# One stage for layer norm, routing, ranks, the row table and ten shared groups, with a fixed table region for each expert

## The reference

```python
x = x + scan_layer(layernorm(x))            # unchanged by this change
xt = layernorm(x)                           # 8192 x 256
scores = softmax(xt @ gate_w.T)             # 15 experts
topk_w, topk_idx = top_k(scores, 3); topk_w /= sum(topk_w) + 1e-20
h = xt @ fc1_w[e].T + fc1_b[e]; xh, g = h[:256], h[256:]
y = sum over the 3 chosen e of topk_w * ((gelu(g) * xh * mult[e]) @ fc2_w[e].T + fc2_b[e])
hs = xt @ s_fc1_w.T + s_fc1_b; xs, gs = hs[:512], hs[512:]
ys = (gelu(gs) * xs * s_mult) @ s_fc2_w.T + s_fc2_b      # the shared expert, every token
x = x + y + ys
```

## Time and profile before

| | us |
|---|---|
| median of 3 runs (1834.9 to 1839.58) | 1835.92 |
| the profiled execution | 1849.06 |
| its span, first to last instruction | 1847.4 |
| routing, first load of `x2` to 724 | 107 |
| ranks, 724 to 752 | 28 |
| shared groups 0 to 9, 752 to 1043 | 291 |
| experts, 1043 to about 1690 | 647 |

### The profile page before, as it was taken

One profiled execution on the slowest core, in us unless ns is written; L12 is line 12 of the kernel. 1 busy time (PEld: TensorE's weight loads), 2 busy tenths in 40 slices (PEclk: granted clock), 3 DMA queues, 4 the chain that ended last, 5 costly groups with the idle time before them and its releaser, 6 DMA issues. The chain is left out here.

```text
span 1847.4 us, 25112 instructions
## 1 busy us (share of the span) xinstructions
PE 1490.6 (81%) x5738; PEld 928.8 (50%) x5738; DVE 1089.6 (59%) x2054; ACT 842.3 (46%) x1420; POOL 1118.8 (61%) x1021
## 2 busy tenths in 40 slices
PE   6883766667666595496888699999999999995997
PEld 2332444444443494253544466666666666663564
DVE  5655999999999486521211444444444444442698
ACT  6887988988998110111111133333333333332210
POOL 6887887888886231576767166666666666662000
PEclk9996888888889555697988899999999999997998
DMA  4433233332231461586873222222222222224895
GB/s 135 141 109 138 71 124 114 126 124 100 97 126 57 150 196 45 132 146 103 154 135 61 59 86 86 89 87 88 88 87 89 86 86 89 89 87 166 290 346 210
DMA packets 138089, 221.23 MB, mean 120 GB/s; under 512 B 21021, under 2 KB 103173, under 8 KB 137989
## 3 DMA queue, kind: packets, MB, share of 16 engines
q1 hardware_dynamic: 100053, 138.17, 24.4%
q0 software_dynamic: 27840, 60.96, 10.5%
q10 hardware_dynamic: 10096, 20.86, 6.0%
HBM read 153.13 MB, written 66.79 MB: 119 GB/s over the span
## 5 line engine op out<-in xcount | busy, mean ns | idle before, releaser
L1697 PE MATMUL bank<-arena_dt,xgT 128*128 x832 | 393.6, 596 | 0.1
L741 POOL TENSOR_TENSOR state<-arena_x,b_all 128x1024 f32<-128x1024 f32 x128 | 301.5, 2365 | 69.7 <-issue 66.3
L765 PE MATMUL bank<-ident,state 128*128 128x128 f32 x1024 | 189.0, 321 | 165.6 <-ACT scaled L678 73.2
L1656 POOL DMA_INDIRECT choice_out<-ye,ids x208 | 205.3, 987 | 163.2 <-DVE ye L1796 159.8
L820 DVE TENSOR_TENSOR_SCAN state<-bank,state 128x1024 f32<-128x1024 f32 x128 | 291.6, 2279 | 5.0 <-POOL state L741 4.9
L1782 DVE TENSOR_TENSOR hid<-bank,arena_x 128x512 f32<-128x512 f32 x208 | 143.9, 692 | 250.2 <-PE bank L1697 250.2
L1647 POOL DMA_INDIRECT xg<-x_norm,tokens x208 | 201.2, 967 | 101.8 <-issue 60.9
L765 PEld LDWEIGHTS bank<-ident,state 128*128 128x128 f32 x1024 | 131.5, 162 | 225.8 <-DVE state L820 123.3
L1536 POOL DMA_INDIRECT row_choice<-choice_all,row_i x192 | 188.9, 984 | 72.2 <-issue 55.1
L1762 ACT ACTIVATE gluT<-bank 128x256 f32<-128x256 f32 x208 | 80.0, 385 | 321.9 <-PE bank L1706 321.9
L1714 PE MATMUL bank<-arena_x,gluT 128*128 x832 | 213.9, 380 | 0.0
(11 more groups left out here) (160 smaller groups left out, 2245.3 us busy)
## 6 DMA issues: line engine op xcount, KB each, us to landing
b_all<-bc_rows SPq DMA_DIRECT2D x64, 512.0 KB, 3.5
arena_x<-choice_out SPq DMA_DIRECT2D x64, 384.0 KB, 7.7
xin<-in_x SPq DMA_DIRECT2D x16, 512.0 KB, 3.9
x_skip<-xin SPq DMA_DIRECT2D x16, 512.0 KB, 2.9
y_acc<-x_skip SPq DMA_DIRECT2D x8, 1024.0 KB, 6.7
x_mid<-y_acc SPq DMA_DIRECT2D x8, 1024.0 KB, 6.5
x<-x_mid SPq DMA_DIRECT2D x16, 512.0 KB, 4.7
x_norm<-xnb SPq DMA_DIRECT2D x16, 512.0 KB, 3.2
```

Of the source, the lines that this page charges most:

```text
L741: pool.tensor_tensor(state[j % STATES][:, :, here], gT[:, :, b, here], b_all[j % BUFS][:, here].unsqueeze(1).to_broadcast([P, KD, TH]), AL ...
L765: last = pe.transpose(bank[:, TURN + (BY_PE * j + q) % 2, i * D + k * P:i * D + (k + 1) * P], state[j % STATES][:, k, t * P:(t + 1) * P], ...
L1656: pool.indirect_dma_start(out=choice_out, out_offset=bass.IndirectOffsetOnAxis(ap=ids[:, j % 2, j // 2:j // 2 + 1], axis=0), in_=ye[c][:], ...
L1697: last = pe.matmul(bank[:, 2 + s, :], xgT[s][:, k, :], w1[:, k, ds(e_no * (2 * F), 2 * F)], start=(k == 0), stop=(k == KD - 1))
```

## The change

Routing, ranks and the ten shared groups become one stage. Its program is written in slots: slot q, from 0 to 39, holds one quarter of a shared group on PE, ACT and DVE (`fc1(q)`, `gelu(q)`, `glu(q)`), and the steps of routing group g stand in slots counted from `turn_slot(g)`: its transposes in that slot, its logits one later, its three best two later, its ranks and rows four later. The ten shared groups are no longer the first ten but `group_of[j]`, spread over the 16, and use the transposed tokens that routing leaves in `xnT`; `xa` is not loaded in this stage. Two running sums (`seen`) replace the one chain over all tiles. Each expert has a region of 8192 rows in the table, so that a group's rows are known before the later groups are, and its 12 scatters follow at once. Where each of the 208 tiles stands is worked out at the end (`tile_row`), and the experts' stage reads its rows by two indirect DMAs. `xm` has one buffer in this stage, not two. The loads of the experts' weights are cut and placed anew: second weights and their biases in slots 1 to 7, first weights in slots 9 to 23, first biases in slots 36 and 39. The expert numbers of the tiles are made at the start of the experts' stage.

```diff
-    row_choice = nc.dram_tensor("row_choice", (XT * P, 1), F32, kind="Internal").ap()
+    row_table = nc.dram_tensor("row_table", ((E + 1) * TILES * P, 1), F32, kind="Internal").ap()
...
+        group_of = [j * GROUPS // G1 for j in range(G1)]
+        group_of += [g for g in range(GROUPS) if g not in group_of]
...
+            SLOTS_ALL = G1 * KS
+            FIRST, LAST = -4, SLOTS_ALL + 2
+            def turn_slot(g):
+                return 5 * g // 2 - 3
+            def routed_at(q):
+                return [g for g in range(GROUPS) if turn_slot(g) == q]
...
+                    def load_xm(j):
+                        wait(sp, stored, 16 * j)
+                        sp.dma_start(xm[:], group_rows(x_mid, group_of[j])).then_inc(xm_loaded, 16)
+                    def store_xm(j):
+                        sp.wait_ge(acc_made, 2 * (j + 1))
+                        sp.dma_start(group_rows(x_mid, group_of[j]), xm[:]).then_inc(stored, 16)
...
+                        j, i = q // KS, q % KS
+                        if i == 2 and 1 <= j < G1:
+                            store_xm(j - 1)
+                            load_xm(j)
...
+                    def scatter(g):
+                        pool.wait_ge(rows_made, g + 1)
+                        for t in range(g * GT, (g + 1) * GT):
+                            wait(pool, c_sent[t % 4], 48 * (t // 4))
+                            for k in range(TOPK):
+                                pool.indirect_dma_start(
...
+                    for g in range(GROUPS):
+                        if g + 3 < GROUPS:
+                            rstds(g + 3)
+                        scatter(g)
...
+                    for q in range(FIRST, LAST):
+                        for g in routed_at(q):
+                            turn(g)
+                        for g in routed_at(q - 1):
+                            logits(g)
+                        for g in routed_at(q - 2):
+                            turn_logits(g)
+                        for g in routed_at(q - 4):
+                            rank(g)
...
+                        if 0 <= q < SLOTS_ALL:
+                            fc1(q)
+                        if j >= 1 and i < 2:
+                            fc2(j - 1, i)
...
+                        if 0 <= q < SLOTS_ALL:
+                            glu(q)
+                        if j >= 1 and i < 2:
+                            add_out(j - 1, i)
+                        for g in routed_at(q - 2):
+                            choose(g)
+                            if g + 3 < GROUPS:
+                                measure(g + 3)
+                        if i == 3 and 0 <= j < G1:
+                            add_bias(j)
...
@@ experts' stage
-                    sp.dma_start(row_ids[:], row_choice.rearrange("(q s p) o -> q s (p o)", s=2, p=P)).then_inc(ids_loaded, 16)
+                    for s in range(2):
+                        pool.indirect_dma_start(
+                            out=row_ids[:, s, :], out_offset=None, in_=row_table.rearrange("(r p) o -> r (p o)", p=P),
...
+                    for e in range(E):
...
+                    dve.wait_ge(expert_step, E + 1)
+                    dve.tensor_copy(tile_expert[:], exp_f[:]).then_inc(expert_step, 1)
```

More of the change, by code:

```diff
@@ L104, in pairwise @@
         def pairwise(eng, n, body):
[L106 to L111, removed]
+            for j in range(n):
                 body(j, j % 2)
@@ L1160, in model_kernel @@
[L1160 to L1163, removed]
+            late, GD = KD * E * D, GT * D
+            x2 = [arena_x[:, late + c * GD:late + (c + 1) * GD].rearrange("p (i d) -> p i d", i=GT) for c in range(4)]
+            xn2 = [arena_x[:, late + (4 + c) * GD:late + (5 + c) * GD].rearrange("p (i d) -> p i d", i=GT)
+                   for c in range(2)]
@@ L1167, in model_kernel @@
+            assert spare + 2 * GT * E <= late + E * 2 * F
+            seen = [sb(f"seen{c}", [P, GT, E]) for c in range(2)]
+            row_f = sb("row_f", [P, GT, E])
+            picked = sb("picked", [P, GT, TOPK])
             ek = sb("ek", [P, TILES, TOPK])
             z_sum = sb("z_sum", [P, TILES])
[L1169 to L1175, removed]
@@ L1193, in _ @@
[L1193 to L1226, removed]
@@ new lines, in logits, with turn_logits @@
+                    def logits(g):
+                        pe.wait_ge(xnT_made, g + 1)
+                        wait(pe, logits_kept, g)
+                        for k in range(KD):
+                            last = pe.matmul(bank[0:E, 3, :], gate[:, k, :], xnT[g % 4][:, k, :], start=(k == 0),
+                                             stop=(k == KD - 1))
+                        last.then_inc(logits_done, 1)
+                    def turn_logits(g):
+                        pe.wait_ge(logitT_made, g + 1)
+                        for i in range(GT):
+                            last = pe.transpose(bank[:, 3, i * (E + 1):i * (E + 1) + E], logitT[:, i * P:(i + 1) * P],
+                                                ident[0:E, 0:E])
+                        last.then_inc(logits_turned, 1)
@@ new lines, in fc2 @@
+                    def fc2(j, p):
+                        pe.wait_ge(glu_made, KS * (j + 1))
+                        wait(pe, acc_made, 2 * j + p)
+                        for i in range(2):
+                            for k in range(KS):
+                                last = pe.matmul(bank[:, 6, i * D:(i + 1) * D],
+                                                 sglu[j % 2][:, k, (2 * p + i) * P:(2 * p + i + 1) * P], sw2[:, k, :],
+                                                 start=(k == 0), stop=(k == KS - 1))
+                        last.then_inc(o_done, 1)
@@ L1574, in _, with normalise @@
-                    pairwise(act, G1, body)
-                    act.wait_ge(w_loaded, (4 * LOADS + 1) * 16)
+                    def normalise(g):
+                        c = g % 4
+                        act.wait_ge(x2_loaded[c], 16 * (g // 4 + 1))
+                        act.wait_ge(off_made, g + 1)
+                        wait(act, xn2_turned, g - 1)
+                        wait(act, xn2_stored[g % 2], 16 * (g // 2))
+                        for i in range(GT):
+                            last = act.activation(xn2[g % 2][:, i, :], x2[c][:, i, :], ACT.Identity,
+                                                  bias=off[c][:, i:i + 1], scale=rstd[c][:, i:i + 1])
+                        last.then_inc(xn2_made, 1)
```

728 lines of the change are left out of this document (386 added, 342 removed).

## The result

The changed kernel takes 1861.63 us (median of four, 1853.06 to 1873.33) where the kernel before took 1835.74 on the same chip: a ratio of 1.0141, 95% interval 1.0084 to 1.0199. The whole interval is above 1, so it is slower. I had forecast 1758, in a range of 1730 to 1795, and given slower 0.04.

What follows compares the result with a forecast made beforehand. POOL's scatters and PE's waits lay side by side, neither starting before the last rank. Overlapped, POOL's chain bounds the stage at 343.5 against 426.4 us, 83 less; minus 5.4 in the experts' stage, 77.6 gained: 1758, range 1730 to 1795.

Steps and rivals of the forecast that it cites:

- The scatters: 260.8 as before: POOL in the new stage: issuing the 192 scatters takes 260.8 us, their 16.7 us of waits for earlier scatters included.
- 260.8 + 24 + 11 + 3: POOL's chain after the first scatter: scatters 260.8 us, statistics steps 24, port holds 11, late rows 3.
- The sum of bytes: DMA load of the new stage: 137 GB/s in 343 us at a share of 0.77, high but not full.
- DVE needs 4.6 of it, so 16.5 are free: Of PE's 21.1 us before it needs the next GLU, 16.5 remain for the store and load of `xm`.
- the slower rival: `xm` alone: nine mean round trips from 28.5 us on bring PE to 421 us, gain gone; chance 0.03.
- PE's 313: PE's end in the new stage, 313 us if nothing else stops it, 30 us ahead of POOL.
- my own sign: In the changed profile, PE's or DVE's longest wait being for the load of `xm` would make the first rival right.
- the first rival: PE held by `xm`: nine round trips of 23.7 us give 1793, only six that meet weights 1771; chance 0.22.
- The weights here come in smaller bursts ... so I take 17 to 20: Round trip of `xm` in the new stage: 17 to 20 us where weights load, absent from slot 24 to 36.
- The landing of the last scatter and the barrier: End of POOL's chain in the new stage: taken as 3.7 us, from a range of 2.7 to 9.0.
- Port holds: DVE's operations on two SBUF operands hold POOL's scatter issues in the new stage: 11 us more.
- 343.5: Forecast length in us of the new stage, set by POOL's chain, against 426.4 before.

Runs made afterwards that it cites:

- more_scatters: The changed kernel with 16 semaphores for the scatters instead of four, so at most 48 scatters under way instead of 12; ratio 1.0244.
- regions_65_best: The changed kernel with regions of 65 tiles, two `xm` buffers, 16 scatter semaphores, and expert numbers made at the end of the stage; ratio 0.9545.

## Why the prediction was wrong

**The step that failed** is the second one on POOL: "The scatters: 260.8 as before". I counted the issues, which did stay at 0.96 us, and did not price that the table's regions now lie 32,768 bytes apart. In the changed kernel the scatters fill 650.8 to 1030.4, 379.6 us, where my terms up to there (260.8 + 24 + 11 + 3) give 298.8: POOL waited 77.8 us for rows, for which I had put 3, and 28.3 for landings instead of 16.7. The distance made a scatter's landing 12.9 us when alone, instead of 3.9 before and 3.3 with 65 tiles. With regions of 65 tiles and nothing else changed the stretch is 313.0 us, and with two buffers as well 294.5. The sum of bytes, 137 GB/s at a share of 0.77, could not show this: the share went up to 1.01 at 142 GB/s.

**`xm`** is where it showed. From "DVE needs 4.6 of it, so 16.5 are free" and a mean trip of 27.6 the slower rival's own rule, 9 x (trip - 16.5) on PE's 313, gives 413 for the 421 at which it set the turn, and the stage took 438.7. By my own sign, DVE's longest wait being for `xm`, the first rival (0.22) and the slower one (0.03) had the right place. Both priced the loss too low, and the distance that made the trips long was in neither; nor is `xm` all of it, as the 413 us without reloads show. "The weights here come in smaller bursts ... so I take 17 to 20" was wrong even by the trace of before: in three stretches of its shared stage (760 to 860, 860 to 940, 940 to 1010) the medians of load and store of `xm` add up to 28.7, 28.3 and 19.4 us. With late scatters in that kernel, and the weights as they were, they add up to 11.1 (7.1 and 4.0).

On two rules of the Trainium skill. "DMA: Bandwidth & Descriptors", section "Latency and other measured facts", has copies between tensors in main memory slow down when the rows lie a large power of two apart, 207 GB/s at 512 KiB and 103 at 4 MiB, and 4 KiB of padding on the 4 MiB bring back 214; the cause is called an inference there. These runs show a loss by the distance at much smaller ones and for 4-byte writes, and 512 bytes of padding did more than 4 KiB (0.9652 and 0.9872). And the estimate that I drew from "SBUF — State Buffer", section "The DMA setup-cost knee", 3.2 us for 512 KB, is near what the stores take with late scatters, 2.9 for `xm` and 3.8 for `x_norm`; the loads of `x2` took 5.7 there.

**The landing of the last scatter and the barrier**, 3.7: measured 20.8 in the changed kernel, 19.3 without the reloads and 15.1 with regions of 65 tiles and two buffers (946.44 + 0.95 to 962.46). The drain of 7.2 us stands in the trace of before, but under other work, and I had not looked for it.

**Port holds**, 11 us more: the scatters' mean is 0.985 us in the changed kernel and 0.995 with regions of 65 tiles and two buffers, 0.984 before. 192 x 0.011 are 2 us. Single holds are real: in the kernel before all seven scatters that began while DVE added `xm` and the bias took 1.21 to 1.83 us; but too few begin so.

**Right**: the first scatter at 38.4 us (41), with 65 tiles and two buffers the 12 statistics steps between the scatters, 2.2 us each in most groups and 26 together (24, for 13), PE's path up to the last sum 303.8 us with late scatters (32 + 258 + 12 + 2 = 304), its full clock there, and the experts' first gather 8.9 us into their stage (9.3), from these rows of the changed kernel's timeline, which answer to the earlier trace rows:

```profile
1050.46 0.32 DVE L1830 TENSOR_SCALAR exp_f<-tile_no,tiles_to 1x208 f32<-1x208 f32 x1 [1.35 <-PEq L114]
...
1059.36 0.98 POOL L1704 DMA_INDIRECT xg<-x_norm,tokens  x1 [5.49 <-DVE tokens L1847]
```

So the plan of the stage holds once the distance is mended. With regions of 65 tiles it lasts 366.8 us, and 0.9652 of 1835.9 is 1772, in the range; with two buffers as well, which I had not planned, 346.9 us and 1751. That this lies so near 343.5 and 1758 is partly luck: the end is 11.4 us longer than my 3.7, and the first scatter (37.3) and the scatters' stretch (294.5) are 3.7 and 4.3 shorter than mine.

## What to carry to other kernels

When a table is filled at several places at about one rate, try another distance of these places: here one tile of padding for each expert, 33,280 bytes instead of 32,768, was worth 4.9%, and distances that 4,096 or 8,192 divides were worse. When work is moved beside other transfers, price the transfers beside it too, and look whether the DMA share and the GB/s still go together: 0.88 at 135 GB/s here, 0.61 at 200 in the same stretch without the scatters. The share alone does not tell the loss, since the fast kernel with two buffers has 0.99 at 147; moving the suspected stream behind the rest showed in one run which one it is. When a wait for a store stands in SP's queue, count what is queued behind it: a second buffer only moved that wait. A last indirect transfer costs its landing and POOL's drain, 15 to 21 us here, once nothing covers them.

## What the runs showed of the hardware

- 192 scatters of 128 x 4 bytes, with nothing beside them: a median landing of 12.9 us with places 32,768 bytes apart and 3.3 with 33,280. That the writes meet in one part of the memory is argued from this; what happens inside the memory no run shows.
- Beside such scatters, which move 0.1 MB in all, a load of 512 KB (`x2`) took 10.3 us instead of 5.7 at 32,768 bytes and 12.8 instead of 5.6 at 33,280 (14.6 with two buffers); a store of 512 KB (`x_norm`) took 11.7 instead of 3.8 and 9.0 instead of 4.1. So the distance relieved the stores, not these loads.
- POOL's drain at the end of the stage with the 192 scatters took 7.16 to 7.17 us in all kernels with four semaphores for them, and 4.48 in the two with 16 (more_scatters and regions_65_best). Why, no run shows.
